# Expert stage of a fused scan-and-MoE kernel: second layer with the rows streaming, and gathered rows turned by VectorE instead of TensorE

## What is computed

```python
x = x + ln(scan_attention(ln(x)))          # gated recurrence, then a 256x256 projection
x = x + ln(ffn(ln(x)))
# ffn, for xf = ln(x) flattened to 16384 rows of D = 256, E = 8 experts, capacity C = 320, H = 1024:
eid  = argmax(softmax(xf @ router_w + router_b))
rank = position of the row among the rows of its expert;  valid = rank < C
h = relu(buf @ w1[e] + b1[e]);  y = h @ w2[e] + b2[e]     # buf: the first 320 rows of each expert
yov = relu(xf @ ow1 + ob1) @ ow2 + ob2                    # every other row
out = y where valid, else yov
```

## Time and profile before

| | |
|---|---|
| median of 3 runs | 1139.37 us (1139.37 to 1139.41) |
| the profiled execution | 1139.46 us |
| its span | 1137.5 us |
| PE, DVE, ACT, POOL busy in the span | 98%, 87%, 68%, 58% |
| granted TensorE clock | 0.996 |
| DMA | 186314 packets, 92.46 MB |

### The profile page before, as it was taken

How to read it: one execution, slowest core, us unless ns; L and a number is a source line. 1 busy time by engine, 2 the same in 40 slices (tenths; PEclk the granted TensorE clock), 3 DMA queues, 4 the chain that set the end, 5 groups by cost and what they waited for, 6 DMA issues and landing times. The chain is left out here.

```text
span 1137.5 us, 24653 instructions
## 1 busy us (share of the span) xinstructions
PE 1118.9 (98%) x7341; PEld 996.5 (88%) x7341; DVE 989.5 (87%) x2795; ACT 772.7 (68%) x1433; POOL 661.6 (58%) x734
## 2 busy tenths in 40 slices
PE   8999999999999999999999999999999999999996
PEld 4788988888888898888888888898889988899996
DVE  6888899899999999998989898999999888688885
ACT  5366676667766667666677666677666776687882
POOL 3556666656666665666666666566666655324443
PEclk9999999999999999999999999999999999999998
DMA  8211043222222222222222222222222220435430
GB/s 259 68 48 57 20 126 80 72 76 56 74 74 74 74 74 73 69 72 70 72 53 72 73 57 72 60 71 74 74 74 74 55 93 20 128 126 175 159 126 31
DMA packets 186314, 92.46 MB, mean 81 GB/s; under 512 B 121403, under 2 KB 182509, under 8 KB 186148
## 3 DMA queue, kind: packets, MB, share of 16 engines
q1 hardware_dynamic: 179108, 86.65, 27.3%
q0 software_dynamic: 7168, 5.34, 1.6%
HBM read 53.82 MB, written 38.76 MB: 81 GB/s over the span
## 5 line engine op out<-in xcount | busy, mean ns | idle before, releaser
L691 ACT ACTIVATE hid<-psH,biasT 128x512 f32<-128x512 f32 (+1 forms) x312 | 202.7, 650 | 206.0 <-PE psH L1432 203.9
L1538 PE MATMUL psY<-W_hi,hid_hi 128*128 128x256 f32 x1168 | 336.1, 288 | 0.3 <-DVE hid_lo L1112 0.2
L1541 PE MATMUL psY<-W_hi,hid_lo 128*128 128x256 f32 x1168 | 330.5, 283 | 0.0
L1540 PE MATMUL psY<-W_lo,hid_hi 128*128 128x256 f32 x1168 | 330.3, 283 | 0.0
L1430 PE MATMUL psH<-xfT_hi,W_hi 128*128 128x512 f32 (+1 forms) x624 | 235.8, 378 | 0.3 <-ACT hid L691 0.2
L1112 DVE TENSOR_TENSOR hid_lo<-hid,hid_hi 128x512 fp32r<-128x512 f32 (+1 forms) x308 | 200.1, 661 | 40.3 <-ACT hid_hi L696 37.0
L1431 PE MATMUL psH<-xfT_lo,W_hi 128*128 128x512 f32 (+1 forms) x624 | 235.0, 377 | 0.0
L1432 PE MATMUL psH<-xfT_hi,W_lo 128*128 128x512 f32 (+1 forms) x624 | 232.6, 373 | 0.0
L1538 PEld LDWEIGHTS psY<-W_hi,hid_hi 128*128 128x128 f32 x1168 | 223.0, 191 | 9.2 <-issue 1.5
L1540 PEld LDWEIGHTS psY<-W_lo,hid_hi 128*128 128x128 f32 x1168 | 223.3, 191 | 6.0
L1541 PEld LDWEIGHTS psY<-W_hi,hid_lo 128*128 128x128 f32 x1168 | 223.1, 191 | 0.0
(11 more groups left out here) (179 smaller groups left out, 2167.5 us busy)
## 6 DMA issues: line engine op xcount, KB each, us to landing
xin<-L_attn_x SPq DMA_DIRECT2D x32, 512.0 KB, 3.5
stage<-L_ffn_w SPq DMA_DIRECT2D x16, 1024.0 KB, 5.5
out<-outt SPq DMA_DIRECT2D x31, 512.0 KB, 2.8
stage<-L_attn_x SPq DMA_DIRECT2D x26, 512.0 KB, 3.5
stage<-tok SPq DMA_DIRECT2D x416, 32.0 KB
xbuf<-zrow SPq DMA_DIRECT2D x1, 2590.0 KB, 16.8
xin<-xbuf SPq DMA_DIRECT2D x8, 259.0 KB, 5.3
stage<-L_ffn_ow SPq DMA_DIRECT2D x2, 1024.0 KB, 8.8
```

The lines of the kernel that those rows point to most:

```text
L691: act.activation(hid[j % 2][:, at:n], psH[:, j % 2, at:n], ACT.Relu, bias=bias).then_inc(s_hid, 1)
L1538: pe.matmul(dst, hi, w[0][:, j, :], start=(j == 0 and (tail or t % 2 == 0)), stop=False, skip_group_check=True)
L1540: pe.matmul(dst, hi, w[1][:, j, :], start=False, stop=False, skip_group_check=True)
L1541: last = pe.matmul(dst, lo_, w[0][:, j, :], start=False, stop=(j == HC - 1), skip_group_check=True)
```

## The change

Three things change in the expert steps, for experts 0 to 6 as the current one or 2 to 7 as the next one.

- **Layer 2 turned** (experts 0 to 6). The weight tile is stationary and the 320 hidden columns move: six matmuls of 320 columns a block, the result with features on partitions in `psY`. VectorE adds b2 as a value per partition into `yT` (two instructions of 128x320), and TensorE, in the next step after its second layer-1 block, transposes `yT` back (six 128x128) into `psA`. The statistics, now after `lo(1)`, and `norm3` read `psA` instead of `ysb`.
- **Rows in squares** (experts 2 to 7). SyncE fetches the rows a second time in pieces of 32 floats by 32 rows with twelve DMAs (`load_blocks`): eight with 320 pieces of 128 bytes, four with the two norm factors of each row, 320 pieces of 8 bytes. GpSimd multiplies and adds (`norm_blocks`, four instructions of 128x320 with two SBUF operands), and VectorE turns the 32x32 squares straight to `psT` (`turn_rows`, two instructions of 128x320, after `lo(5)`). VectorE's `norm2` and TensorE's `transposes1` fall away for these experts.
- The bias rows of b2 are loaded for the transposed biases at the start, one DMA more.

```diff
             def load_blocks(e):          # SyncE, new
+                rows = xbuf.rearrange("(e b r) w -> e r b w", r=SQ, b=C // SQ)[i * 2 + v]
+                if blocked(grp(i, v, -1)):
+                    sp.wait_ge(s_tok2, cnt(grp(i, v, -1), 1, 1) + NG)
+                for a in range(P // SQ):
+                    quad = slice(a * SQ, (a + 1) * SQ)
+                    sp.dma_start(sblk[quad], rows[:, :, D + 1:D + 3]).then_inc(s_xblk[v], 16)
+                    for n in range(DC):
+                        sp.dma_start(xblk[quad, n, :].rearrange("p (b c) -> p b c", c=SQ),
+                                     rows[:, :, n * P + a * SQ:n * P + (a + 1) * SQ]).then_inc(s_xblk[v], 16)
 # SyncE, in estep, between load_w1(far) and load_w2(far)
+                if blocked(far):
+                    load_blocks(far)
 # GpSimd, new; in estep behind deviation(3, prev), ahead of rows_of and keep_rows
+            def norm_blocks(e):
+                pool.wait_ge(s_xblk[v], landed((i - 1, v), 3 * (P // SQ)))
+                pool.wait_ge(s_T1, cnt(e, 2, 0) + 2 * NG)
+                for k, (src, op) in enumerate(((xblk, ALU.mult), (tok2_blk, ALU.add))):
+                    if k:
+                        pool.wait_ge(s_scaled, cnt(e, DC, -DC))
+                    for n in range(DC):
+                        last = pool.tensor_tensor(tok2_blk[:, n, :]..., src[:, n, :]...,
+                                                  sblk[:, :, k:k + 1].to_broadcast([P, C // SQ, SQ]), op)
+                last.then_inc(s_tok2, 1)
 # VectorE, new
+            def turn_rows(e):
+                dve.wait_ge(s_tok2, cnt(e, 1, 1) + NG)
+                for c in range(DC):
+                    dve.transpose(psT[:, c, 0:C], tok2_blk[:, c, :]).then_inc(s_T1, 1)
+            def result_turned(e):
+                dve.wait_ge(s_l2, cnt(e, HC, HC) + HC * NG)
+                for m in range(DC):
+                    dve.tensor_scalar(yT[:, m, 0:C], psY[:, m, 0:C], biasT[:, bass.ds(col, 1)], None, ALU.add)
 # VectorE, in estep
-                    if j == 0:
-                        if live(prev, E):
-                            read_rows3(prev, ET, NG)
                     if j == 1:
                         if live(prev, E):
+                            read_rows3(prev, ET, NG)
                             moments(3, prev, ET, NG)
-                        if j == 2:
+                        if j == 2 and not blocked(nxt):
                             norm2(nxt, xe, ET, NG)
+                        if j == 5 and blocked(nxt):
+                            turn_rows(nxt)
-                    result(now, b2_b[:, bass.ds(ei, 1), :], ET, NG)
+                    result_turned(now)
 # TensorE, new, and in estep
+            def layer2_turned(g, j, w):
+                for m in range(DC):
+                    cols = slice(m * P, (m + 1) * P)
+                    pe.matmul(dst, w[0][:, j, cols], hi, ...)
+                    pe.matmul(dst, w[0][:, j, cols], lo_, ...)
+                    last = pe.matmul(dst, w[1][:, j, cols], hi, ...)
+                    if j == 1 and live(grp(i, u, -1), E):
+                        turn_result(grp(i, u, -1))          # six transposes yT -> psA
-                    if j == HC - 1 and live(nxt, E):
+                    if j == HC - 1 and live(nxt, E) and not blocked(nxt):
                         transposes1(nxt, ET, NG)
-                        layer2(now, j - 2, ET, W2[u], EL1)
+                        layer2_turned(now, j - 2, W2[u])
```

More of the change, by code:

```diff
@@ L57, in piped, with blocked @@
     return not isinstance(g[0], int) or 2 * g[0] + g[1] >= PIPED
+def blocked(e):
+    return not isinstance(e[0], int) or 2 <= 2 * e[0] + e[1] < E
 def shared2(g):
@@ L103, in sandwich_kernel @@
         BG = OB1 + HC
+        B2 = BG + DC
         ident = sb("ident", [P, P])
@@ L148, in by_feature @@
             return buf[:].rearrange("p t d -> p (t d)").rearrange("p (c n) -> p c n", c=DC)
+        yT = by_feature(att)
+        xblk = keep[:].rearrange("p c n -> p (c n)")[:, 0:DC * C].rearrange("p (n c) -> p n c", c=C)
+        sblk = ngx[:, 0, 0:2 * (C // SQ)].rearrange("p (b k) -> p b k", k=2)
+        tok2_blk = tok2[:].rearrange("p t d -> p (t d)")[:, 0:DC * C].rearrange("p (n c) -> p n c", c=C)
         W_raw = [outt[n][:, DC:2 * DC, :] for n in range(2)]
@@ L276, in sandwich_kernel @@
         s_xe = sems("s_xe")
+        s_xblk = sems("s_xblk")
+        s_scaled = sem("s_scaled")
         s_oidx = sem("s_oidx")
@@ L280, in sandwich_kernel @@
         s_tail_z = sem("s_tail_z")
+        s_yt = sem("s_yt")
         s_tail_out = sem("s_tail_out")
@@ L642, in estep @@
                     deviation(3, prev, ET, NG)
+                if live(nxt, E) and blocked(nxt):
+                    norm_blocks(nxt)
                 if live(prev, E):
@@ L718, in norm3 @@
                 act.wait_ge(s_nm[3], cnt(g, 1, 1) + base)
-                act.wait_ge(s_y, cnt(g, 2, 2) + 2 * base)
+                if base:
+                    act.wait_ge(s_out, cnt(g, 1, 0) + base)
+                else:
+                    act.wait_ge(s_y, cnt(g, 2, 2))
                 for t in range(t0, n):
-                    last = act.activation(ysb[:, t, :], ysb[:, t, :], ACT.Identity, bias=nmr[3][:, t:t + 1],
+                    last = act.activation(ysb[:, t, :], (psA_t if base else ysb)[:, t, :], ACT.Identity, bias=nmr[3][:, t:t + 1],
                                           scale=rstd[3][:, t:t + 1])
@@ L1129, in read_rows3 @@
             def read_rows3(g, n, base=0, t0=0):
-                dve.wait_ge(s_y, cnt(g, 2, 2) + 2 * base)
-                read_rows(3, lambda t: ysb[:, t, :], n, t0)
+                if base:
+                    dve.wait_ge(s_yt, cnt(g, 1, 1))
+                    read_rows(3, lambda t: psA_t[:, t, :], n)
+                else:
+                    dve.wait_ge(s_y, cnt(g, 2, 2))
+                    read_rows(3, lambda t: ysb[:, t, :], n, t0)
+            def result_turned(e):
+                dve.wait_ge(s_l2, cnt(e, HC, HC) + HC * NG)
+                if live(grp(*e, -1), E):
+                    dve.wait_ge(s_yt, cnt(e, 1, 0))
+                dve.sem_inc(s_held_v, 1)
+                for m in range(DC):
+                    col = (e[0] * 2 + e[1]) * DC + B2 + m
+                    dve.tensor_scalar(yT[:, m, 0:C], psY[:, m, 0:C], biasT[:, bass.ds(col, 1)], None, ALU.add)\
+                        .then_inc(s_y, 1)
             def stats3(g, n, base=0, t0=0):
@@ L1370, in estep @@
                     lo(now, j, C, EL1, tail=not live(nxt, E))
-                    if j == 0:
+                    if j == 0 and not live(prev, E):
+                        read_rows3(last_group, TG)
+                    if j == 1:
                         if live(prev, E):
                             read_rows3(prev, ET, NG)
-                        else:
-                            read_rows3(last_group, TG)
-                    if j == 1:
-                        if live(prev, E):
                             moments(3, prev, ET, NG)
@@ L1422, in _ @@
                 last.then_inc(s_wT, 1)
-            pe.wait_ge(s_w["bias"], 48)
+            pe.wait_ge(s_w["bias"], 64)
             pe.transpose(psH[:, 0, 0:P], bias_rows[:], ident[:]).then_inc(s_wT, 1)
@@ L1544, in layer2, with turn_result @@
                 return last
+            def layer2_turned(g, j, w):
+                pe.wait_ge(s_hid_lo, cnt(g, HC, j + 1) + EL1)
+                hi, lo_ = hid_of(j, 0)[:, 0:C], hid_of(j, 1)[:, 0:C]
+                for m in range(DC):
+                    cols = slice(m * P, (m + 1) * P)
+                    dst = psY[:, m, 0:C]
+                    pe.matmul(dst, w[0][:, j, cols], hi, start=(j == 0), stop=False, skip_group_check=True)
+                    pe.matmul(dst, w[0][:, j, cols], lo_, start=False, stop=False, skip_group_check=True)
+                    last = pe.matmul(dst, w[1][:, j, cols], hi, start=False, stop=(j == HC - 1), skip_group_check=True)
+                last.then_inc(s_l2, 1)
+            def turn_result(e):
+                pe.wait_ge(s_y, cnt(e, 2, 2) + 2 * NG)
+                if live(grp(*e, -1), E):
+                    pe.wait_ge(s_z, cnt(e, 1, 0) + NG)
+                for t in range(ET):
+                    for m in range(DC):
+                        last = pe.transpose(psA_t[:, t, m * P:(m + 1) * P], yT[:, m, t * P:(t + 1) * P], ident[:])
+                last.then_inc(s_yt, 1)
             def step(i, u):
@@ L1720, in estep @@
                         layer1(now, j, C, W1[u], EL1)
+                        if j == 1:
+                            turn_result(grp(i, u, -1))
                         if j == 3:
```

23 lines of the change are left out of this document (19 added, 4 removed).

## The result

| | before | after |
|---|---|---|
| median, same chip | 1139.43 us (6 runs, 1139.37 to 1139.6) | 1148.28 us (6 runs, 1148.23 to 1148.38) |
| ratio, 95% interval | | 1.0076 (1.0066 to 1.0087) |
| span of the profiled execution | 1137.5 us | 1146.4 us |
| granted clock | 0.996 | 0.997 |
| PE, DVE, ACT, POOL busy | 98, 87, 68, 58% | 97, 87, 68, 58% |

What follows compares the result with a forecast made beforehand. VectorE's chain was to replace TensorE as the bound: 16.05 + 0.44 + 0.82 + 0.04 + 1.15 gives an 18.5 us period. Six periods add 11.1, with -0.55 and +0.66 +11.2 on 1139.46: 1150.7 us, range 1142 to 1158.

Steps and rivals of the forecast that it cites:

- VectorE's chain: Expert step through `norm3`, `lo(4)` and `xfT_lo`: 16.05 us before, 17.35 after without GpSimd's hold, past TensorE's 14.7.
- layer-2 block: TensorE, turned layer 2: six matmuls of 320 columns take 0.88 us for 1.08, 1.6 us off a step.
- statistics' move: VectorE, statistics behind `lo(1)`: factors, `norm3`, the weights' high part and `lo(4)` come later, +0.44 us a step.
- `turn_rows`, a step: VectorE behind `lo(5)`, in the stretch without a gap: two square transposes of 0.41 us, +0.82 us (0.76 to 0.96).
- GpSimd's four: Products and sums hold VectorE through the shared port and delay `lo(4)`: +1.15 us a step, between nothing and +3.1.
- last `lo` to the next layer 1: Step end: not counted; the end of `xfT_lo` was taken as when the next layer 1 may start.
- period: Step from one expert's layer 1 to the next: 18.5 us, six of them 111.0 for 99.87, +11.1 us.
- expert 0: First expert's step, VectorE's chain as it is: only 0.6 us of TensorE's saving can be cashed, -0.55 us taken.
- expert 7: Last expert's step: gets the six transposes and no turned layer, +0.66 us on TensorE, which bounds it.
- twelve fetches, w2 behind them: SyncE: issue takes 7.8 to 9.8 us, w2 lands about S' + 9.2; hidden with 1.4 us to spare.
- the rival of the late fetch: SyncE: pieces cost twice, issues take 18 us, w2 lands late, some 4 us an expert: 1172 us; chance 0.08.

Runs made afterwards that it cites:

- run 1: Layer 2 turned but no squares, statistics behind `lo(1)`, against the kernel before: 1140.95 us, ratio 1.001, period 16.83.
- run 6: Layer 2 turned, no squares, statistics behind `lo(0)`, `norm3` and residual sum unmoved, against the kernel before: 1136.93 us, ratio 0.9978, period 16.18.
- run 5: Changed kernel with only the statistics moved back behind `lo(0)`: 1144.30 us, ratio 1.0043 to the kernel before, period 17.41.
- run 4: Changed kernel without VectorE's two square transposes an expert, semaphore raised instead: 1144.03 us, ratio 1.0037 to the kernel before, period 17.33.
- run 3: Changed kernel without GpSimd's four products and sums, rows not normalized: 1146.29 us, ratio 1.0055 to the kernel before, period 17.57.
- run 8: Changed kernel, squares kept, with statistics behind `lo(0)`, `norm3` after block 4, residual sum after `lo(5)`: 1139.48 us, ratio 0.9999 to the kernel before.
- run 10: Changed kernel with statistics behind `lo(0)`, `norm3` after block 4, residual sum after `lo(5)`, without GpSimd's four: 1139.20 us, ratio 0.9999 to the kernel before.
- the late order: Statistics behind `lo(0)`, `norm3` after block 4, residual sum after `lo(5)`; in the changed kernel with squares, 1139.48 us.
- run 7: Layer 2 turned, no squares, statistics behind `lo(0)`, `norm3` and residual sum one block later, against the kernel before: 1135.78 us, ratio 0.9968.
- run 11: Layer 2 turned, no squares, statistics behind `lo(0)`, `norm3` after block 4, residual sum after `lo(6)`, against the kernel before: 1140.46 us, ratio 1.0008.

## Why the prediction was right, and where it was off

The claim was that VectorE's chain takes over from TensorE and grows, so that TensorE's saved work is not cashed. Runs 1 and 6 show it: the same saving of 1.6 us is worth nothing with the statistics behind `lo(1)` (period 16.83) and 0.47 us a step with them behind `lo(0)` (16.18 against 16.65). The mechanism was right; the size was right in part because its errors went opposite ways, as told below.

| step | forecast | measured |
|---|---|---|
| layer-2 block | 0.88 us | 0.88 (1086.19 to 1087.07) |
| statistics' move, a step | +0.44 | +0.67 (run 5) |
| `turn_rows`, a step | +0.82 | 0.82 from start to start (0.91 to its end); +0.75 (run 4) |
| GpSimd's four, a step | +1.15 | +0.51 (run 3) |
| last `lo` to the next layer 1 | not in the chain | +0.22 to 0.26 |
| period | 18.5 | 18.08 |
| expert 0 | -0.55 | -0.36 |
| expert 7 | +0.66 | +0.67 |
| twelve fetches, w2 behind them | hidden | hidden |

**The statistics, priced too low.** The move was put at 0.44 us a step and costs 0.67 (run 5). The forecast was worked out for expert 4, so it is read there; VectorE, then ScalarE:

```profile
1068.55 0.49 DVE L1171 TENSOR_TENSOR hid_lo<-hid,hid_hi 128x320 fp32r<-128x320 f32 x1 [0.23 <-ACT hid_hi L747]
...
1070.20 0.31 DVE L1008 BATCH_NORM_AGGREGATE mv<-st 128x2 f32<-128x6 f32 x3 [0.15 <-DVE st L1001]
...
1075.57 0.96 DVE L1171 TENSOR_TENSOR hid_lo<-hid,hid_hi 128x320 fp32r<-128x320 f32 x1
```

```profile
1072.62 1.48 ACT L775 ACTIVATE ysb<-psA,nmr,rstd 128x256 f32<-128x256 f32 x3 [1.23 <-POOL nmr L487]
```

S is 1064.66. `lo(1)` started at S + 3.89 for a forecast 3.74, and the moments waited 0.15 us for the statistics' own semaphore, which `lo(1)` had covered before. So `norm3` started at S + 7.96 for 7.62. It took 1.48 us for 1.59, reading PSUM, and `lo(4)` started at S + 10.91, where the forecast had 10.68 without a hold: 0.23 late. That little of this shows in the sum is luck. The forecast took S + 10.24, of expert 4, for every step, while the mean before was 10.13; the mean after is 10.75, 0.07 above 10.68.

**GpSimd, the mis-sized term.** The four by tile, ns min/median/max:

```profile
L648 POOL TENSOR_TENSOR tok<-keep,ngx x12: 727/804/975, 1018.0 to 1109.5; 128x320 f32<-128x320 f32 x12
L648 POOL TENSOR_TENSOR tok<-tok,ngx x12: 730/956/1184, 1019.9 to 1111.0; 128x320 f32<-128x320 f32 x12
```

The shortest, 0.73 us, is below the 0.79 that I took from the length; the longer ones stand beside VectorE's own. In expert 5 the products began at S + 7.72 and ended at S + 9.29, in VectorE's wait; the sums ended at S + 11.34, forecast S + 11.8. From the weights' low part to `lo(4)` it is 0.92 us with the four and without (run 3): the stretch of the first lay in the 0.23 us wait for ScalarE's high part. Only `lo(4)`'s 0.48 us count, against 0.51 measured by run 3 and 1.15 forecast. Of the miss of the period, 18.5 - 18.08 = 0.42, this makes 0.64, and the next point takes 0.22 back; the 0.07 of the statistics and the 0.07 by which `turn_rows` cost less cancel.

The Trainium skill (SBUF — State Buffer, section "SBUF: two separate sides") has the pair of ports as a lock held for a whole instruction. The traces agree with 0.97 for 0.49 us of `lo(4)`, with and without the four. They add that a hold costs little where VectorE would have waited: run 8 with holds of 1.56 us a step and run 10 without have the same ratio, 0.9999, and their expert 5 differs by 0.14 us.

**The link that was missed.** I took the end of `xfT_lo` as what lets the next layer 1 start. It is not the last: `lo(7)` ended at 1099.89, the eighth layer-2 block started at 1099.94 and took 1.00, and layer 1 followed at 1100.94, while `xfT_lo` had ended at 1100.68. The seventh block, held to 1098.94 by `lo(6)`, ended at the same time as `lo(7)`, so either of the two would have set this start. The same in run 1 (1.03 behind `lo(7)`) and run 3 (1098.03 to 1099.08). So TensorE's idle time shows ahead of layer-2 blocks with `hid_lo` as releaser (0.35, 0.48 and 0.66 us in expert 5) and not, as the prediction had it, ahead of the first layer 1 with `xfT_lo`. It also means that before the change VectorE's chain was closer than the 0.6 to 0.7 us that I read. `lo(7)` of expert 6 in the kernel before, VectorE's timeline:

```profile
1108.66 0.48 DVE L1112 TENSOR_TENSOR hid_lo<-hid,hid_hi 128x320 fp32r<-128x320 f32 x1
```

It ended at 1109.14, a block of nine takes 1.08, and layer 1 came at 1110.70, so 0.48 us was left (0.41 in expert 4 by the same sum). Expert 0 gained 0.36 and not 0.55.

**SyncE.** w2's issue in expert 1, behind the first twelve fetches; then the first and the last of the twelve in expert 5, and w2's behind them:

```profile
1014.17 0.41 SPq L342 DMA_DIRECT2D stage<-L_ffn_w  x1
...
1094.56 0.33 SPq L424 DMA_DIRECT2D ngx<-xbuf  x1
...
1100.13 0.84 SPq L426 DMA_DIRECT2D keep<-xbuf  x2
1101.42 0.39 SPq L342 DMA_DIRECT2D stage<-L_ffn_w  x1
```

In expert 5 they took 6.4 us, under the 7.8 by count, and w2 went out at S' + 0.5 for a forecast S' + 3.1. The first twelve took 7.8 us, and w2 went out at S' + 3.70 in expert 1, later than forecast. No wait of ScalarE for `stage` shows in the changed kernel; in the late order one does (runs 8 and 10), so the rival of the late fetch was not far off in expert 1.

**The parts together.** The ratios are 1.001 for the turned layer alone, 1.0047 for the squares alone and 1.0076 for both. The remaining 0.0019, some 2 us, comes only together. The intervals of the three ratios leave that open; the periods say the same: +0.18 and +0.93 alone, +1.43 together. Alone, the first part of the chain's growth is used up by the slack behind TensorE. The squares lose in every order tried. With everything late (runs 7 and 8) they cost 3.7 us more than TensorE's own transposes. By the rows, they take 0.66 us from TensorE, which isn't the bound once the chain is, and put 0.82 us on VectorE in the stretch that has none to spare; run 4 measured that price, 0.75 us, in the changed kernel's own order.

## What to carry to other kernels

Ahead of a change that takes work off an engine that is 98% busy, follow the next chain through the other engines to its end, to 0.1 us, and up to the instruction that stands ahead in the queue of the engine that is to start: here it lay half a microsecond behind, so that of 1.6 us saved a step 0.5 were cashed, and 0.6 once `norm3` and the residual sum came a block later (-0.32%). Work put on VectorE in its stretch without a gap costs about its full time (0.75 of 0.82 us in run 4), stretches put where it waits cost little (0.14 of 1.56 us between runs 8 and 10). An operation moved back by one block in a program's order counts as a cost wherever it heads such a chain.

## What the runs showed of the hardware that was not expected

- VectorE instructions stretched beside GpSimd's are often harmless: 1.56 us a step went with no difference in the time and 0.14 us in expert 5 (runs 8 and 10), 0.74 us with 0.51 (run 3), while moving one from `lo(6)` to `lo(7)` (1.12 for 0.48 us) went with some 4.5 us in all (run 11 against run 7, each against its own kernel before), 0.44 us a step of it with no other delay.
- VectorE's square transpose of 128x320 float32 into PSUM took 0.476 to 0.516 us, 0.41 from start to start, and ran at that length beside GpSimd's DMA instructions and beside its copy to `x1` (run 8, expert 5: 0.90 us for the two).
- A DMA issue of 320 pieces of 128 bytes took 0.41 to 0.46 us of SyncE in expert 5 (half of a pair's 0.82 to 0.91), against 0.65 for one of 256 pieces in the main loop: the count of pieces alone does not set it.
